# Thirty-four extra row gathers in the setup stage of a two-layer graph network

## What is computed

```python
h = jnp.maximum(_layernorm(x), 0.0)
h_nodes = _mlp2(h, node_W1, node_b1, node_W2, node_b2)
h_edges = _mlp2(edge_attr, edge_W1, edge_b1, edge_W2, edge_b2)
msgs = _mlp2(concatenate([h_nodes[dst], h_nodes[src], h_edges]), msg_W1, ...)
agg = segment_sum(msgs, dst) / maximum(counts, 1.0)
x = x + layernorm(h + _mlp2(concatenate([h, agg]), upd_W1, ...)) * ln_g + ln_b
h = jnp.maximum(_layernorm(x), 0.0)
g = (h @ W).reshape(N, 4, 32)
alpha = softmax over the edges of one dst of leaky_relu(a_src[src] + a_dst[dst])
x = x + segment_sum(g[src] * alpha, dst) + bias
```

## Time and profile before

| What | Value |
|---|---|
| Median of 3 runs | 4668.64 us (4656.42 to 4673.68) |
| The profiled execution's own time | 4664.53 us |
| Its span, first to last instruction | 4662.7 us |
| Mean granted TensorE clock | 0.798 of full speed |
| TensorE matmul busy | 3890.3 us (83%) |
| GpSimd (POOL) busy | 3331.3 us (71%), 3234 instructions |
| ScalarE busy | 2672.2 us (57%) |
| VectorE busy | 2382.2 us (51%) |

### The profile page before, as it was taken

How to read it: one execution, slowest core, us unless ns; L and a number is a source line. 1 busy time by engine, 2 the same in 40 slices (tenths; PEclk the granted TensorE clock), 3 DMA queues, 4 the chain that set the end, 5 groups by cost and what they waited for, 6 DMA issues and landing times. The chain is left out here.

```text
span 4662.7 us, 130488 instructions
## 1 busy us (share of the span) xinstructions
PE 3890.3 (83%) x40200; PEld 3499.5 (75%) x40201; DVE 2382.2 (51%) x9720; ACT 2672.2 (57%) x4890; POOL 3331.3 (71%) x3234
## 2 busy tenths in 40 slices
PE   3788888888888888887748988999999999899992
PEld 2577777777777777775538888898989888888882
DVE  5522222222222222222757676777777767677767
ACT  3555555555655555563436666666666666666662
POOL 1377777777777777775657777777777777777772
PEclk9799999999899999997867677667776767776766
DMA  3422222222222222222532222222222222222223
GB/s 114 139 54 52 53 54 51 54 52 53 54 51 54 53 52 54 51 53 58 151 99 52 51 51 52 51 53 53 52 53 53 52 51 51 51 52 52 51 51 114
DMA packets 309081, 285.67 MB, mean 61 GB/s; under 512 B 127646, under 2 KB 229812, under 8 KB 309044
## 3 DMA queue, kind: packets, MB, share of 16 engines
q0 software_dynamic: 100352, 160.76, 16.4%
q1 hardware_dynamic: 206786, 121.71, 9.1%
q10 hardware_dynamic: 1906, 2.77, 0.2%
HBM read 249.16 MB, written 35.83 MB: 61 GB/s over the span
## 5 line engine op out<-in xcount | busy, mean ns | idle before, releaser
L655 POOL DMA_INDIRECT a_G<-Htab,a_idx x1568 | 1654.7, 1055 | 494.8 <-issue 477.6
L655 POOL DMA_INDIRECT p_rows<-Btab,p_idx x1568 | 1493.4, 952 | 496.6 <-issue 477.6
L1514 PE MATMUL a_psA<-a_GP,a_S 128*128 128x132 f32 x4704 | 975.9, 389 | 0.7 <-DVE a_GP L1437 0.7
L1514 PEld LDWEIGHTS a_psA<-a_GP,a_S 128*128 128x128 f32 x4704 | 899.4, 290 | 6.5 <-DVE a_GP L1437 0.9
L832 DVE TENSOR_TENSOR p_z<-p_psZ,p_rows 128x512 f32<-128x512 f32 x294 | 198.7, 690 | 1258.6 <-SPq L764 1223.2
L1487 ACT CAST a_S<-a_Sb 128x512 f32<-128x512 bf16 x588 | 633.2, 1130 | 62.2 <-PE a_psA L1514 61.2
L953 PE MATMUL p_psA<-p_msg,p_S 128*128 128x65 f32 x4704 | 599.3, 289 | 21.6 <-ACT p_S L895 21.6
L953 PEld LDWEIGHTS p_psA<-p_msg,p_S 128*128 128x128 f32 x4704 | 581.8, 205 | 25.1 <-issue 25.0
L890 ACT ACTIVATE p_msg<-p_z 128x512 f32<-128x512 f32 x294 | 180.9, 630 | 710.3 <-DVE p_z L832 705.1
L935 PEld LDWEIGHTS p_psZ<-wc,p_s 128*128 128x128 f32 x2352 | 344.2, 213 | 323.2 <-issue 312.9
L895 ACT CAST p_S<-p_Sb 128x1024 f32 (+1 forms) x294 | 550.7, 1972 | 0.0
(11 more groups left out here) (220 smaller groups left out, 5243.1 us busy)
## 6 DMA issues: line engine op xcount, KB each, us to landing
p_ea<-in_ea SPq DMA_DIRECT2D x196, 256.0 KB
p_rows<-Btab,p_idx POOLq DMA_INDIRECT x1568
a_G<-Htab,a_idx POOLq DMA_INDIRECT x1568
Htab<-arena SPq DMA_DIRECT2D x14, 476.0 KB, 3.7
n_x<-in_x SPq DMA_DIRECT2D x14, 448.0 KB, 4.1
hkeep<-n_h SPq DMA_DIRECT2D x14, 448.0 KB, 4.9
hTkeep<-n_hT SPq DMA_DIRECT2D x14, 448.0 KB, 4.1
u_hT<-hTkeep SPq DMA_DIRECT2D x14, 448.0 KB, 4.3
```

Of the source, the lines that this page charges most:

```text
L655: pool.indirect_dma_start(out=rows[:, u * C + c, :], out_offset=None, in_=table, in_offset=bass.IndirectOffsetOnAxis(ap=idx[u][:, c:c + 1] ...
L1514: m = pe.matmul(psA[v][:, 0:HR], S32[v][:, c, :], GP[v][:, c, :], start=c == 0, stop=c == C - 1)
```

## The change

Stage 1 gets two scratch tiles: `pidx`, 128 rows of eight source indices, and `prow`, room for 34 gathers of rows of `x`. ACT loads `pidx` ahead of all its other loads. POOL, when the identity matrix is done, waits for `pidx`, issues 34 gathers and waits until all have landed. The number of rows differs: each of 128, 127, 126, 125, 124, 123, 122, 119, 115, 114, 112, 120, 96, 64, 32, 16 and 8 comes twice. Nothing reads `prow`.

```diff
     iota_i = sb("iota_i", [P, P * C], I32)
+    counts = [n for n in (128, 127, 126, 125, 124, 123, 122, 119, 115, 114, 112, 120, 96, 64, 32, 16, 8) for _ in range(2)]
+    pidx, prow = sb("pidx", [P, C], I32), sb("prow", [P, len(counts), D])
+    s_pidx, s_prow = sem("c_pidx"), sem("c_prow")
...
         @block.scalar
         def _(act):
             raw, enda, rowa = dst
+            act.dma_start(pidx[:, :], t["src"][0:P, :]).then_inc(s_pidx, 16)
             act.dma_start(enda[:, :], t["dstend"].rearrange("o (q r) -> (o q) r", r=2)).then_inc(s_dst, 16)
...
             pool.affine_select(out=k["ident"][:, :], in_=k["ident"][:, :], compare_op=ALU.not_equal, fill=1.0,
                                base=0, pattern=[[-1, P]], channel_multiplier=1).then_inc(s_id, 1)
+            pool.wait_ge(s_pidx, 16)
+            for i, n in enumerate(counts):
+                pool.indirect_dma_start(
+                    out=prow[0:n, i, :], out_offset=None, in_=t["x"],
+                    in_offset=bass.IndirectOffsetOnAxis(ap=pidx[0:n, i % C:i % C + 1], axis=0)).then_inc(s_prow, 16)
+            pool.wait_ge(s_prow, 16 * len(counts))
```

## The result

| What | Before | After |
|---|---|---|
| Median of 3 runs | 4668.64 us | 4705.55 us (4701.98 to 4709.73) |
| Ratio of the runs | | 1.0086, 95% interval 1.0063 to 1.0108 |
| Span of the profiled execution | 4662.7 us | 4703.7 us |
| POOL busy | 3331.3 us | 3374.3 us |

The changed kernel is 36.9 us slower, by the interval between 29 and 50 us. The forecast was 26.8 us and 4696 us. Two sets of later runs (`again`, `all128`, `up16` and `split`; `mark`, `split_b` and `all128_b`) were taken on two chips where every kernel, the one before too, took 7030 to 7205 us, with pauses of POOL in the passes of up to 19.5 us at an "issue" (`again`), so only the ratios of these sets and the rows of their stages 1 and 2 are used.

What follows compares the result with a forecast made beforehand. POOL's gather pace was taken to bound both passes, and POOL's chain to set stage 1. 42.5 + 0.2 - 0.3 + 2.9 + 1.6 + 0.5 - 20.3 - 0.3 = +26.8 us gave 4696 us, range 4684 to 4738 us.

Steps and rivals of the forecast that it cites:

- What bounds the kernel, and the slack: POOL's pace of gathers sets both edge passes, 4100 of 4663 us; in stage 1 POOL has 16.9 us of slack.
- The start: Stage 1: the index load costs POOL nothing, so its gathers begin at about 2.9 us, after the identity matrix.
- 34 x 1.25 us: POOL's gathers in stage 1: each takes 0.95 us plus a 0.30 us gap whatever its rows, 42.5 us in all.
- rival B: Stage 1 gathers: awkward counts are dear, only engines dividing the count take part; up to +87 us, 4755 us; chance 0.33.
- lowest form: Rival B with POOL held until the one engine is through: 8 us above the forecast sum, +35 us, 4704 us.
- The half-fixed form of rival B: Stage 1 gathers: half of POOL's time fixed, half by one engine's rows; about +52 us, 4721 us.
- The landing: End of stage 1: the last gather lands 1.6 us after its issue, as the index load did, at 46.9 us.
- The end of the block: From stage 1's last instruction to POOL's first of stage 2: 0.51 us, so stage 2 starts at 47.4 us.
- The 0.3 us back in stage 2: Stage 2: VectorE no longer waits for `raw`, which will long be there, so 0.3 us comes back.
- the prediction's own sign of being wrong: POOL's chain in stage 1 shorter than 38 or longer than 50 us, or the passes changing their pace.
- Rival A: Stage 1 gathers: price follows the rows, +19.3 us (0.41%); half fixed, half by rows +23.0 us; chance 0.20 together.
- Rival C: Both passes: uneven gathers leave POOL's queues in another state; 10 ns a gather give +58 us, 4727 us; chance 0.05.

Runs made afterwards that it cites:

- again: The changed kernel once more, unaltered; ratio 1.0048 (1.0018 to 1.0078) against the kernel before.
- all128: The changed kernel with all 34 gathers of 128 rows; ratio against the kernel before 1.0030, and 1.0036 in the repeat `all128_b`.
- up16: The changed kernel with each of the 34 counts rounded up to a multiple of 16; ratio 1.0035 against the kernel before.
- split: The changed kernel with 12 cheap gathers in stage 1, the 22 others in stage 2; ratio against before 0.9997, and 1.0052 in the repeat `split_b`.
- mark: The changed kernel with a small POOL memset between the wait for all landings and the stage's end; ratio 1.0104 against the kernel before.
- serial: The changed kernel with 20 gathers instead of 34, POOL waiting for each landing; landings took 1.5 us (8 rows) to 4.8 to 5.3 us (127 rows); no total given.

## Why the prediction came out as it did

**What bounds the kernel, and the slack: right.** POOL's pace is unchanged in the passes (median 944 against 947 ns, gap 0.30 us), stage 1 is set by POOL's chain, and moving the gathers into slack takes 28 of 37 us away up to the start of stage 3. Of the arithmetic, 1568 x (952 + 300) ns is 1963 us and not 1968; with the gap of 305 ns of the earlier trace rows it is 1971, and the pass measured 1970.

**The start: 0.5 us short.** POOL was taken to go on at 2.9 us and did at 3.44. The gap behind the identity matrix was 0.53 us.

**34 x 1.25 us: the term that was mis-sized.** I took 0.95 us for every count. The chain from the first to the end of the last was 49.8 us (3.44 to 53.23), not 42.4. The 780 rows on busiest engines instead of 272 are 508 x 13.5 ns = 6.9 us of the 7.4. This is rival B's mechanism, with its divisors as stated, but at 13.5 ns a row and not at its bounds of 118 ns or of a POOL that is held until 30.5 ns a row have passed. Its lowest form, +8 us, came near in size for another reason: it wanted 122 rows at 1.9 and 127 at 3.9 us, and 124 rows at no surcharge. Measured were 1.66, 2.56 and 1.29. The half-fixed form of rival B was also mis-added: 34 x 0.475 + 780 x 0.0594 us are 62.5 us of work, which gives +57 and not +52 us. The choice of the forecast over rival B was a choice between 26.8 and 35 us, and the even dealing read from the earlier trace rows spoke for the right one.

**The landing: right.** 1.6 us were taken, 1.43 measured in `mark`.

**The end of the block: a term left out.** 0.51 us had been read from a stage without gathers. The DRAIN of POOL, 82 ns for each of the 34 gathers, was put at nothing and took 2.84 us. The idle time behind the last gather was 4.44 us, not 2.1; with the landing 0.2 us shorter, the end of the block was 2.5 us longer.

**The 0.3 us back in stage 2: half of it.** Stage 2 took 39.33 us up to POOL's first of stage 3, where it had been 39.51.

The sum of stage 1 and 2 becomes 26.8 + 0.5 + 7.4 + 2.3 + 0.1 = 37.1 us, against 37.2 in the trace and 36.9 in the medians. The forecast was low by 10 us, and the range from 4684 to 4738 us held the result.

How much of this was luck: the direction and the place were reasoned rightly, but the forecast's fixed price was wrong, and the range held because rivals on both sides had widened it. The measured 4706 us lie beside the 4704 of rival B's lowest form, which got there with too high a price per row and without the DRAIN. By the prediction's own sign of being wrong, a chain longer than 50 us, it passed by 0.2 us.

**Rival A** fell: the fixed part is 0.84 of 0.95 us, and its half-fixed form as well. **Rival C** is not seen in the message pass (1970.2 against 1970.1 us). In the attention pass 2.8 us remain which neither theory accounts for, and every kernel with gathers in stage 1 had more there, up to 18 us in `serial`, in one profiled execution each. So rival C is not excluded for that pass.

## What to carry to other kernels

Price a gather by the rows on its busiest DMA engine: on POOL that was 0.84 us and 13.5 ns for each. For a short series add 82 ns for each gather at the DRAIN that ends the block (34 at most here). And round an awkward count up to a multiple of 16: 128 rows cost 0.94 us, 127 cost 2.56, and with all 34 counts rounded up the stage ended 8 us earlier while moving more data. Before adding work to an engine, take its slack in that stage alone from the timeline, and check what else runs in the place you move it to, since gathers beside wide operations of VectorE took up to 0.9 us longer. And do not read the cost of a stage's end from a stage without gathers.

## What was not expected of the hardware

- Issuing 127 rows takes POOL 2.55 us, and after every seventh such gather in a row it stands still, 5.3 to 6.9 us, until all of them have landed.
- A gather of 127 rows makes 272 packets where one of 128 makes 32: one engine takes all rows, and each of the other 15 gets as many entries of 4 bytes as that one has rows (`serial`).
- Every gather of stage 1 cost POOL another 82 ns in the DRAIN at the end of the block, 2.84 us for 34, however many rows it had, and even when each landing had been waited for by itself (`mark`, `serial`).
